# Local attention: masking, query norm and row maximum in one fused VectorE operation per 128x128 block, exponentials in place, and new orders on four engines

## The reference: what is computed

```
q = l2norm(q) * qs; k = l2norm(k) * ksc; q, k = rotary_xpos(q, k)      # 8 heads of 64
sim = einsum('bhwid,bhwjd->bhwij', bq * 8.0, bk)     # windows of 64 queries; own and previous window of keys
sim = where((i < j) | (i > j + 64) | (j == -1), -max, sim)
out = einsum('bhwij,bhwjd->bhwid', softmax(sim), bv)
x = x + out @ wo
```

## Time and profile before

| | |
|---|---|
| median of 3 runs | 2307.49 us (2306.52 to 2309.47) |
| profiled execution | 2311.73 us, its span 2309.9 us |
| busy in the span | PE 94%, ACT 77%, DVE 73%, POOL 62% |
| granted PE clock, mean | 0.977 |
| L373 (the maximum), first to last, call 1 | 762.05 to 1015.24 us |
| call 2 | 1105.31 to 1358.92 us |
| call 3 | 1624.55 to 1877.91 us |
| call 4 | 1969.61 to 2222.90 us |

### The profile page before, as it was taken

How to read it: one execution, slowest core, us unless ns; L and a number is a source line. 1 busy time by engine, 2 the same in 40 slices (tenths; PEclk the granted TensorE clock), 3 DMA queues, 4 the chain that set the end, 5 groups by cost and what they waited for, 6 DMA issues and landing times. The chain is left out here.

```text
span 2309.9 us, 67166 instructions
## 1 busy us (share of the span) xinstructions
PE 2175.3 (94%) x22598; PEld 1606.6 (70%) x22598; DVE 1691.0 (73%) x3594; ACT 1782.4 (77%) x6112; POOL 1432.2 (62%) x1432
## 2 busy tenths in 40 slices
PE   6987999999698999999999999899999999999999
PEld 4984666665696788864788864675788864788863
DVE  5554888886554889973899974575899963899964
ACT  4774888986575999982899982556999982999982
POOL 4663777773663788860788860572788850888850
PEclk8997999999799999999999999999999999999999
DMA  6111000000113000000000000000000000000000
GB/s 248 43 40 42 2 0 0 0 1 24 40 43 120 9 9 7 9 0 5 9 9 7 9 1 0 2 0 6 9 9 7 9 0 5 9 9 7 9 1 37
DMA packets 22566, 45.93 MB, mean 20 GB/s; under 512 B 5344, under 2 KB 13792, under 8 KB 22048
## 3 DMA queue, kind: packets, MB, share of 16 engines
q1 hardware_dynamic: 17440, 34.01, 4.4%
q0 software_dynamic: 4992, 10.23, 1.5%
HBM read 24.44 MB, written 11.40 MB: 16 GB/s over the span
## 5 line engine op out<-in xcount | busy, mean ns | idle before, releaser
L279 POOL TENSOR_TENSOR space<-space 128x512 f32<-128x512 f32 x256 | 325.7, 1272 | 268.5 <-DVE space L382 268.1
L274 POOL TENSOR_TENSOR space<-space 128x512 f32<-128x512 f32 x256 | 267.6, 1045 | 126.1 <-ACT space L315 125.9
L329 ACT ACTIVATE space<-psum,space 128x128 f32<-128x128 f32 x1024 | 337.0, 385 | 1.7 <-DVE space L373 1.7
L1011 POOL TENSOR_TENSOR space<-space 128x256 f32<-128x256 f32 (+1 forms) x256 | 221.4, 886 | 85.2 <-DVE space L1113 83.1
L176 PE MATMUL psum<-big,space 128*128 128x256 f32 x1024 | 266.1, 382 | 6.8 <-issue 3.4
L268 POOL TENSOR_TENSOR space<-space 128x512 f32<-128x512 f32 x256 | 266.9, 1042 | 7.9 <-DVE space L353 7.3
L373 DVE TENSOR_REDUCE space<-psum 128x4 f32<-128x512 f32 x256 | 177.1, 692 | 98.0 <-PE psum L191 93.7
L1057 ACT ACTIVATE space<-psum,space 128x128 f32<-128x128 f32 (+1 forms) x512 | 210.3, 442 | 1.8 <-DVE space L1106 1.7
L329 ACT ACTIVATION_READ_ACCUMULATOR space<-psum,space 128x1 f32 x1024 | 201.8, 197 | 0.0
L176 PEld LDWEIGHTS psum<-big,space 128*128 128x128 f32 x1024 | 174.6, 190 | 28.4 <-issue 15.2
L676 ACT ACTIVATE big<-psum,wt 128x512 f32<-128x512 f32 (+1 forms) x96 | 65.4, 686 | 152.0 <-PE psum L653 151.9
(11 more groups left out here) (196 smaller groups left out, 5483.3 us busy)
## 6 DMA issues: line engine op xcount, KB each, us to landing
big<-early SPq DMA_DIRECT2D x1, 6944.0 KB, 27.5
rows<-space SPq DMA_DIRECT2D x16, 256.0 KB, 2.4
z<-token_y SPq DMA_DIRECT2D x16, 256.0 KB, 5.3
space<-z SPq DMA_DIRECT2D x64, 64.0 KB, 1.9
space<-z SPq DMA_DIRECT2D x64, 63.8 KB, 2.1
big<-late SPq DMA_DIRECT2D x1, 3114.0 KB, 13.7
x<-x_t SPq DMA_DIRECT2D x4, 512.0 KB, 5.2
x_final<-x SPq DMA_DIRECT2D x8, 256.0 KB, 2.1
```

The source lines that it names most:

```text
L274: pool.tensor_tensor(x, x, rn[:, (j - 1) % 2, :].unsqueeze(2).to_broadcast([P, 8, LD]), ALU.mult).then_inc(scaled, 1)
L279: pool.tensor_tensor(t3[:, j % 2, :], t1[:, j % 2, :], t2[:, j % 2, :], ALU.add).then_inc(summed, 1)
L329: ins = act.activation(pr[:, j % 2, h, t * P:(t + 1) * P], s_ps[h][:, t * P:(t + 1) * P], ACT.Exp, bias=nm[:, j % 2, h, t:t + 1], accum_ou ...
L1011: ins = pool.tensor_tensor(x, x, rl[:, ee % 2, t, :].unsqueeze(2).to_broadcast([P, 2, c1 - c0]), ALU.mult)
```

## The change

The mask is no longer put into PSUM ahead of QK, and q is no longer multiplied by its norm. QK starts fresh in the score banks (its first piece is now 128 columns wide instead of 64), and DVE then runs four fused operations, one for each head and half of the queries: each reads 128x128 scores from PSUM and 128x128 of the mask, adds them, multiplies by the query's norm `rn` (one value per partition, read through a pointer), writes the result to `pr` in SBUF, and reduces it with min into one column of `nm`. The table for q has the sign turned (-8 for 8), so that the minimum is the negated maximum. ACT's exponentials work on `pr` in place with scale -1, and their row sums go to SBUF. POOL multiplies only k by `rn` (128x256). PE transposes q before the probabilities (it waits for `summed` only) and k after them. ACT copies v at the second place of a step, one pair later, and computes the logarithm ahead of the squares. DVE adds the output's halves one step later and earlier within the step.

```diff
@@ tensor_body @@
                 pe.wait_ge(qk_ready, S0 + u + 1)
-                pe.wait_ge(masked, S0 + u + 1)
-                for w, q0, spans in ((0, 0, ((0, 0, WIN),)), (1, LD, ((0, 0, P),)), (0, P, ((P, P, WIN), (P + WIN, WIN, WIN))), (1, P + LD, ((P, P, P),))):
+                if at_least(u, 1):
+                    pe.wait_ge(nm_ready, S0 + u)
+                for w, q0, spans in ((0, 0, ((0, 0, P),)), (1, LD, ((0, 0, P),)), (0, P, ((P, P, WIN), (P + WIN, WIN, WIN))), (1, P + LD, ((P, P, P),))):
...
+            u = s - 1
+            if runs(u, U):
+                pe.wait_ge(summed, S0 + u + 1)
...
+                for t in range(2):
+                    nc.tensor.transpose(qkT_ps[:, t * P:(t + 1) * P], t3[:, (j - 1) % 2, t * T:t * T + P], g.ident32)
...
+            u = s - 1
+            if runs(u, U):
+                pe.wait_ge(scaled, S0 + u + 1)
+                for t in range(2):
+                    ins = nc.tensor.transpose(qkT_ps[:, T + t * P:T + (t + 1) * P], t3[:, (j - 1) % 2, t * T + P:(t + 1) * T], g.ident32)
+                ins.then_inc(turned, 1)
@@ gpsimd @@
-                    pool.tensor_tensor(x, x, rn[:, (j - 1) % 2, :].unsqueeze(2).to_broadcast([P, 8, LD]), ALU.mult).then_inc(scaled, 1)
+                    x = t3[:, (j - 1) % 2, :].rearrange("p (t n h d) -> p t n h d", t=2, n=2, h=2)[:, :, 1]
+                    by = rn[:, (j - 1) % 2, :].rearrange("p (t n h) -> p t n h", t=2, n=2)[:, :, 1]
+                    pool.tensor_tensor(x, x, by.unsqueeze(3).to_broadcast([P, 2, 2, LD]), ALU.mult).then_inc(scaled, 1)
@@ scalar_body @@
                 for h in range(2):
+                    act.wait_ge((nm_first, nm_ready)[h], S0 + u + 1)
                     for t in range(2):
-                        ins = act.activation(pr[:, j % 2, h, t * P:(t + 1) * P], s_ps[h][:, t * P:(t + 1) * P], ACT.Exp,
-                                             bias=nm[:, j % 2, h, t:t + 1], accum_out=ls[:, h, t:t + 1])
+                        x = pr[:, j % 2, h, t * P:(t + 1) * P]
+                        ins = act.activation(x, x, ACT.Exp, scale=-1.0, bias=nm[:, j % 2, h, t:t + 1], accum_out=ls[:, j % 2, h, t:t + 1])
@@ vector_body @@
-                dve.tensor_copy(s_pair, band).then_inc(masked, 1)
...
             u = s - 2
             if only is None and runs(u, U):
+                dve.wait_ge(g.tabled, 8)
                 dve.wait_ge(s_ready, S0 + u + 1)
-                dve.tensor_reduce(nm[:, j % 2, :, :], s_pair.rearrange("p h (t n) -> p h t n", t=2), AX.X, ALU.max, negate=True).then_inc(nm_ready, 1)
+                if at_least(u, 2):
+                    dve.wait_ge(ptp_ready, S0 + u - 1)
+                for h in range(2):
+                    for t in range(2):
+                        cs = slice(t * P, (t + 1) * P)
+                        ins = dve.tensor_tensor_reduce(pr[:, j % 2, h, cs], s_ps[h][:, cs], g.band_q[:, cs], rn[:, j % 2, 4 * t + h:4 * t + h + 1], FAR,
+                                                       ALU.add, ALU.min, nm[:, j % 2, h, t:t + 1])
+                    ins.then_inc((nm_first, nm_ready)[h], 1)
```

More of the change, by code:

```diff
@@ L294, in scalar_body @@
                 act.activation(qk[:, j % 2, :], qkT_ps, ACT.Copy).then_inc(qk_ready, 1)
+            u = s - 1
+            if only is None and runs(u, U):
+                act.wait_ge(vp_ready, S0 + u + 1)
+                if at_least(u, 4):
+                    act.wait_ge(ol_ready, S0 + u - 3)
+                act.activation(v[:, (j - 1) % CH, :, :].rearrange("p a b -> p (a b)"), v_ps, ACT.Copy).then_inc(v_ready, 1)
             u = s - 4
@@ L300, in scalar_body @@
                 act.activation(pt[:, j % 2, :, :].rearrange("p h n -> p (h n)"), pt_ps, ACT.Copy).then_inc(pt_ready, 1)
+            u = s - 1
+            if only is None and runs(u, U):
+                act.wait_ge(ss_ready, S0 + u + 1)
+                act.activation(lnn[:, (j - 1) % 2, :], ss[:, (j - 1) % 2, :], ACT.Ln, scale=float(2 ** 20), bias=g.tiny[:, 0:1]).then_inc(ln_ready, 1)
             if begins(s, only):
@@ L352, in vector_body @@
                     dve.wait_ge(normed, S0 + u - 1)
-                dve.reciprocal(rl[:, (j - 3) % 2, :, :], ls).then_inc(rl_ready, 1)
-            u = s - 2
-            if only is None and runs(u, U):
-                if is_first(u):
-                    prev.free(dve, 3)
-                    prev.free(dve, 4)
-                dve.tensor_copy(s_pair, band).then_inc(masked, 1)
+                dve.reciprocal(rl[:, (j - 3) % 2, :, :], ls[:, (j - 3) % 2, :, :]).then_inc(rl_ready, 1)
             u = s - 1
@@ L404, in free @@
     def free(eng, bank):
[L405 removed]
+        last = (rotated, qk_ready, o_ready, nm_ready, nm_ready, pt_ready, o_ready, z_ready)
         eng.wait_ge(last[bank], B0 + B if bank == 7 else S0 + U)
```

66 lines of the change are left out of this document (28 added, 38 removed).

## The result

The changed kernel takes 2394.28 us (median of 4 runs, 2393.45 to 2399.4), the kernel before 2308.23 us in the runs beside it (2306.52 to 2309.47): a ratio of 1.0381, 95% interval 1.0368 to 1.0394. It is 86 us slower.

What follows compares the result with a forecast made beforehand. Bound: the ring over ACT, POOL and PE (4.04 us), a second through DVE at 3.77. The latter becomes 3.16 + 1.36 = 4.52, 0.50 above 4.02: 126 us over 252 periods plus 2 for call ends, 2435 us; range 2345 to 2500.

Steps and rivals of the forecast that it cites:

- the ring over ACT, POOL and PE: Norm of q and k, ACT's copy through POOL's product to PE's transposes: 4.04 us a step, falling to 3.2.
- a second one close under it: QK, DVE's maximum and rotary products, projection, back to QK: needs 3.77 us, 0.25 of slack in 4.02.
- its own pace of 3.96: PE's instruction list: 3.96 us from projection to projection almost without a pause, its work kept by the change.
- the ring QK, fused operations, rotary products, projection: Path through DVE and PE after the change: 3.16 + 4x, 4.52 us a step, 0.50 above 4.02.
- the forecast proper: Whole program with x from 0.31 to 0.37: 2405 to 2465 us, chance 0.50.
- x: On DVE, time from one fused operation's start to the next: taken as 0.34 us, between 0.26 and 0.45.
- the rival "the write costs nothing": DVE's one-column write free or both parts cheaper: x 0.25 to 0.30, 35 to 86 us slower, 2342 to 2393; chance 0.22.
- If pairs cost 0.26: DVE's fused operation with its write at 0.26 us: mechanism stands, size falls to about 45 us.
- ACT's list: ACT's instructions of one step after the change: 4.01 us, or 3.93 with each of four pairs rounded down.
- The third ring: QK, second fused operation, ACT's four exponentials and copy, back to QK: 3.55 + x = 3.89 us, below 4.52.
- POOL's product: POOL's multiplication by the norm halves, 128x256 for 128x512: about 0.52 us less of 1.04.
- The signs: New profile: L177 idle 0.3 to 0.6 us, L404 never waiting, pairs 0.34 apart, PE's share in stretches below 92%.

Runs made afterwards that it cites:

- before_log_first: Kernel before with only ACT's logarithm moved ahead of the squares; 2304.74 us, ratio 0.9964 to the kernel before.
- extra_in_ring: Changed kernel plus a fifth fused operation between the third and fourth, behind DVE's wait for QK; 2462.81 us, ratio 1.0673 to the kernel before.
- extra_before_wait: Changed kernel plus a 200-column addition of constants on DVE ahead of its wait for QK; 2399.39 us, ratio 1.0400 to the kernel before.
- two_wide_fused: Changed kernel with one 128x256 fused operation per head for two of 128x128, second query half using the first's norm and maximum; 2324.24 us.
- narrow_piece: Changed kernel with QK's first piece 64 columns wide again except in a call's first step; 2390.32 us, ratio 1.0341 to the kernel before.
- no_row_sums: Changed kernel with ACT's exponentials giving no row sums, softmax not normalised; 2389.21 us, ratio 1.0352 to the kernel before.
- pe_order_of_before: Changed kernel with PE's transposes of q and k both back behind the value projection; 2400.12 us, ratio 1.0378 to the kernel before.
- product_first: Changed kernel with the first rotary product ahead of DVE's wait for QK, ACT's squares waiting for it; 2421.01 us, ratio 1.0486 to the kernel before.

## Why the prediction was right, and where it was off

**What bounded the kernel before** held: the ring over ACT, POOL and PE, with a second one close under it. The trace of before bears it out: PE's transposes L254 start 0.05 to 0.06 after the end of POOL's L274 in all 256 steps. So PE's list was not running at its own pace of 3.96, as the prediction had it, but was held back a little in each step. before_log_first, which takes a little off this ring, was faster by about 8 us. One thing was overlooked: 4.02 is a mean. Most steps took 3.93 to 3.99, one of eight 4.10, and one of eight 4.25 or more, in which PE's projection started some 0.2 late after a wait for which the profile names no releaser. In the usual step the second ring (3.77) had 0.20 of slack, not 0.25.

**The mechanism** held. The old ring fell away (POOL's k product waits for ACT's L335 only 10.8 us in all, the last figures of its row below), and the ring QK, fused operations, rotary products, projection took over. extra_in_ring, extra_before_wait and two_wide_fused show it from three sides. (That ACT copies v earlier and DVE adds the halves earlier had no run of its own; neither is on the measured ring, which accounts for the whole period.)

The row of the k product among the groups of the changed kernel (busy us, mean ns of one, idle us before it and what ended it):

```profile
L285 POOL TENSOR_TENSOR space<-space 128x256 f32<-128x256 f32 x256 | 157.7, 616 | 10.8 <-ACT space L335 10.8
```

**The sum** came out at 4.52 a step and 2435 us, and 4.365 and 2394.28 were measured, inside the stated range (2345 to 2500) but below the forecast proper (2405 to 2465). The 2 us that it added for the ends of the calls did not show: outside the stretches the kernel became 5 us shorter. Term by term, measured in the step shown above:

| term | predicted | measured |
|---|---|---|
| start of QK to the first DVE operation | 0.71 | 0.86 |
| four fused operations, 4x | 1.36 | 1.09 |
| L404 to L406 | 0.60 | 0.60 |
| L406 to its end | 0.68 | 0.69 |
| its end to the projection | 0.14 | 0.05 |
| projection to QK, with the wait's part | 1.03 | 1.07 |
| sum | 4.52 | 4.36 |

The mis-sized term is x: "I take 0.26 + 0.08 = 0.34". The main part is 0.27, as the pointer operation's row said (0.26); the 0.08 for the one-column write was wrong. The accumulator's read starts at the same time as the next fused operation (884.27 and 884.27), and the pair takes 0.27 where the pointer operation without any read took 0.26, so the read adds 0.01 at most. I had worked from ACT, whose write costs 0.05 to 0.10 on top; DVE's does not behave so.

This is the rival "the write costs nothing", x from 0.25 to 0.30, which had 2342 to 2393 and a chance of 0.22. The measured 2394 lies just above it. The sentence "If pairs cost 0.26, the mechanism stands and the size falls to about 45 us" named nearly the right x and the wrong size: with x = 0.27 the sum gives 3.16 + 1.09 = 4.25, 58 us, and 86 were measured, because the hop from QK grew by 0.15, which I had given 0 to 0.05. It was luck that this second error went the other way and took back half of the first.

Some 0.05 of the longer hop from QK is the wider piece (narrow_piece: 0.81 for 0.86). The rest lies between QK's end at 883.85 and the first fused operation at 883.99, 0.14, where the maximum started 861.95 to 861.99, 0.04 after QK's end. The new operation stands behind waits for several semaphores and the old one waited for one; that the number of waits is the reason is argued from the trace and was not tried. So the cause of 0.10 a step, some 25 of the 86 us, stays open; only its place is shown. The hop into the projection was 0.14 in the one row that the prediction had the earlier trace rows; in the changed kernel it is 0.05 or 0.06 in 210 steps and 0.14 or 0.15 in 36. The errors, -0.27, +0.15, +0.01, -0.09 and +0.04, add up to the -0.16.

**The fixed part, estimated and measured.** The prediction drew an estimate of 0.21 for a main operation and 0.29 for a pair from the Trainium skill (Vector Engine (DVE) Microarchitecture Reference, Measured stream behaviour on trn2). For a pair it was nearer than my 0.34, for 0.27 was measured. Its 1.04 ns a column agrees with the wide operation (0.13 for 128 columns), and its 75 ns an instruction, counted twice, with the 0.14 of a pair. The split does not agree: the pointer operation without a read took 0.26, which leaves it a fixed part of 0.13 by itself, and next to nothing for the read. The rule of the Trainium skill (VectorE: DVE Perf Modes, Rules for kernel authors) to minimise the number of operations agrees with two_wide_fused, where two fused operations fewer brought 70 us.

**ACT's list** was put at 3.93 to 4.01. In the step shown L305 starts at 881.86 and again at 886.27, 4.41 apart; 0.40 of it goes to the wait for L213 and 0.11 to the one for the second fused operation, which leaves 3.90 (an exponential with its row sum costs 0.38 where I assumed 0.40). The third ring was put at 3.89: in the profile after, L305 ends 3.71 after QK's start, and with the hop of 0.16 it needs 3.87. no_row_sums shows that it does not decide.

**POOL's product** takes 0.616 for 1.04, 0.43 saved where I took 0.52: half the elements are not half the time. It changed nothing, since that ring had slack.

**The signs.** L177 waits for L406 in nearly every step: right, but for 0.2 to 0.3 us and not 0.3 to 0.6. L404 never waits: right. Pairs 0.34 apart: wrong, 0.27. PE's share in the stretches below 92%: wrong, 1034.04 / 1100.05 = 94%, because the period grew less. The order of the transposes on PE was given no term, and pe_order_of_before confirms it.

## What to carry to other kernels

Before work is taken off the ring that decides, add up the next ring; here it had 0.20 to 0.25 us of slack, and the change took a copy that ran in front of a wait, where it was free, and put its work behind that wait, where each 0.01 us costs 2.5 us in 252 steps. Work behind such a wait is to be priced by the number of operations as well as by columns: 0.14 of the 0.27 us of each was fixed. And a reordering that cuts a ring needs each new wait followed once around: all versions with the product ahead cut the ring, and each closed another one (on average 4.11, 4.45, 4.34 and 4.44 a step) that no engine's busy share foretold. It also pays to look at more than one step: an operation that comes every fourth step added 0.33 to such a ring in product_first, and the one step first read did not show it.

## What the runs showed of the hardware that was not expected

- DVE's read of the accumulator into SBUF (0.08 long) starts together with the next operation. From one fused operation to the next it is 0.271, against 0.26 for a pointer operation without a read the earlier trace rows, so the read adds 0.01 at most. ACT's read of its accumulator does add: 0.050 when the exponential reads PSUM and the sum goes to PSUM, 0.092 when both are in SBUF, and 0.10 with the source in PSUM and the sum in SBUF.
- An exponential of 128x128 with a pointer bias takes 0.250 to its read out of PSUM and 0.291 out of SBUF.
- Where DVE waited for one semaphore (L373 before) it started 0.04 after PE's end, where it waited for several (L395) 0.14 after it. The two are also different operations, and no run separates the causes.
- The wider first piece of QK made the group take 0.72 for 0.67, and the group behind it started 0.500 after QK for 0.40 to 0.43 before.
